# A third set of the second sequence in seven block products, with its LoRA products, sums and high and low parts moved

## What is computed

```python
# conditioning, per sequence b with its expert e = ids[b]
h = relu(x @ (wi + 2 * common_wi_b @ common_wi_a + 2 * experts_wi_b[e] @ experts_wi_a[e]).T)   # 256 -> 1024
y = h @ (wo + 2 * common_wo_b @ common_wo_a + 2 * experts_wo_b[e] @ experts_wo_a[e]).T         # 1024 -> 256
# router: the mean over the tokens decides
p = softmax(y.mean(tokens) @ gate_w); two largest, shares w = p / sum
# experts
out = x + sum over the two e of w[e] * (gelu(y @ w1[e] + b1[e]) @ w2[e] + b2[e])
```

## Time and profile before

| | us |
|---|---|
| median of 3 runs | 266.91 |
| lowest to highest | 265.99 to 267.07 |
| the profiled execution | 265.94 |
| its span, first to last instruction | 264.2 |
| PE busy | 260.0 (98%) |
| VectorE, ACT, POOL busy | 174.3, 174.8, 160.7 |
| DMA, expert weights, issue to landing (median) | 2.8 |

### The profile page before, as it was taken

One profiled execution on the slowest core, in us unless ns is written; L12 is line 12 of the kernel. 1 busy time (PEld: TensorE's weight loads), 2 busy tenths in 40 slices (PEclk: granted clock), 3 DMA queues, 4 the chain that ended last, 5 costly groups with the idle time before them and its releaser, 6 DMA issues.

```text
span 264.2 us, 3622 instructions
## 1 busy us (share of the span) xinstructions
PE 260.0 (98%) x1156; PEld 212.8 (81%) x1156; DVE 174.3 (66%) x284; ACT 174.8 (66%) x279; POOL 160.7 (61%) x192
## 2 busy tenths in 40 slices
PE   8999999999999999999999999999999999999995
PEld 4778888888878888888888888888888888888884
DVE  1882867376998636657594866658856567665665
ACT  3857365455466289888976887676777677774650
POOL 2267997933398977897549999456366366331100
PEclk9999999999999999999999999999999999999999
DMA  6987120201032102211202112203202206000004
GB/s 187 382 322 244 35 79 0 84 1 40 0 124 79 51 28 80 82 22 59 83 0 63 60 38 79 79 0 83 79 2 79 78 4 200 0 0 2 0 1 159
DMA packets 11139, 19.76 MB, mean 75 GB/s; under 512 B 2000, under 2 KB 2256, under 8 KB 10992
## 3 DMA queue, kind: packets, MB, share of 16 engines
q1 hardware_dynamic: 10544, 18.61, 21.5%
q10 hardware_dynamic: 576, 0.92, 1.0%
HBM read 17.43 MB, written 2.10 MB: 74 GB/s over the span
## 4 chain that ended last, share of the span: by engine, by line
PE 98%; DVE 0%; issue 0%
PE out_ps L762 16%; PE out_ps L759 16%; PE out_ps L758 16%; PE hid_ps L758 15%; PE hid_ps L759 14%; PE hid_ps L762 14%; PE hid_ps L959 2%; PE hid_ps L798 1%; PE out_ps L888 1%; PE hid_ps L802 1%; PE hid_ps L806 1%; PE hid_ps L910 1%; PE hid_ps L900 1%; DVE x_sb L1271 0%; DVE y_sb L1159 0%
## 5 line engine op out<-in xcount | busy, mean ns | idle before, releaser
L413 POOL TENSOR_TENSOR up_lo<-up_raw,up_hi 128x512 fp32r<-128x512 f32 x41 | 53.0, 1311 | 37.1 <-ACT up_hi L573 36.9
L758 PE MATMUL out_ps<-hid_hi,down_hi 128*128 128x512 f32 x190 | 74.0, 390 | 0.0
L762 PE MATMUL out_ps<-hid_hi,down_lo 128*128 128x512 f32 x190 | 74.0, 389 | 0.0
L759 PE MATMUL out_ps<-hid_lo,down_hi 128*128 128x512 f32 x190 | 74.0, 389 | 0.0
L758 PE MATMUL hid_ps<-act_hi,up_hi 128*128 128x512 f32 x166 | 64.9, 391 | 0.0
L759 PE MATMUL hid_ps<-act_lo,up_hi 128*128 128x512 f32 x166 | 64.7, 390 | 0.0
L762 PE MATMUL hid_ps<-act_hi,up_lo 128*128 128x512 f32 x166 | 64.6, 389 | 0.0
L605 ACT ACTIVATE hid_ps<-hid_ps,bias_sb 128x512 f32<-128x512 f32 x64 | 42.2, 659 | 29.1 <-DVE hid_ps L1080 18.0
L1054 DVE SCALAR_TENSOR_TENSOR hid_lo<-hid_ps,mix,hid_hi 128x512 fp32r<-128x512 f32 x64 | 47.9, 748 | 20.3 <-ACT hid_hi L619 19.7
L419 POOL TENSOR_TENSOR down_lo<-down_raw,down_hi 128x512 fp32r<-128x512 f32 x24 | 32.4, 1349 | 37.2 <-ACT down_hi L583 37.2
L619 ACT ACTIVATE hid_hi<-hid_ps,mix 128x512 fp32r<-128x512 f32 x64 | 44.1, 690 | 4.7
(11 more groups left out here) (98 smaller groups left out, 241.9 us busy)
## 6 DMA issues: line engine op xcount, KB each, us to landing
up_raw<-in_w SPq DMA_DIRECT2D x16, 256.0 KB, 2.8
down_raw<-in_w SPq DMA_DIRECT2D x16, 256.0 KB, 2.6
lora_raw<-in_lora SPq DMA_DIRECT2D x10, 256.0 KB, 4.8
down_raw<-in_woT SPq DMA_DIRECT2D x8, 256.0 KB, 3.8
up_raw<-in_wiT SPq DMA_DIRECT2D x7, 256.0 KB, 4.2
outT<-x_sb SPq DMA_DIRECT2D x6, 256.0 KB, 3.5
x_sb<-in_x1T SPq DMA_DIRECT2D x1, 1024.0 KB, 7.6
x_sb<-in_x0bT SPq DMA_DIRECT2D x1, 512.0 KB, 4.0
```

Of the source, the lines that this page charges most:

```text
L413: ins = eng.tensor_tensor(up_lo[:, n, cols], up_raw[:, n, cols], f32(up_hi[:, n, cols]), ALU.subtract)
L758: eng.matmul(out, w_h, a_h, start=start, stop=False, skip_group_check=onto)
L759: eng.matmul(out, w_h, a_l, start=False, stop=False, skip_group_check=onto)
L762: return eng.matmul(out, w_l, a_h, start=False, stop=stop, skip_group_check=onto)
```

## The change

Set 6 becomes a seven-product set too, so that sets 4, 5 and 6 are. What goes with it:

- The up pair of set 6 is made in set 4 (it was in set 5) and that of set 7 in set 5 (it was in set 6). VectorE's merges go with them, and the order of `PRODUCTS` with both.
- POOL makes in set 4 also the weight sums of set 6, ahead of the low part of down set 4, and the low part of up set 6, now eight blocks, directly behind it and so ahead of the router's terms and the LoRA lot of set 7. In set 5 come the first two sums of the output of sequence 0 (they waited for the router's picks and now for its maximum), the low parts of up set 7 and of down set 5. In set 6 come the other two sums, and two of the `raw_low` parts, which VectorE made.
- ACT copies in set 4 the high part of up set 6, in set 5 that of up set 7. The high parts of the output of sequence 0 (`raw_high`) and the first of its sums (`sum_high`) go from set 6 to set 5.
- VectorE makes in set 6 no `raw_low`; two stand in set 7, beside the four `sum_low`. The router's second pick and the shares stand in set 6 between the additions of the seven products.

```diff
-    PLAIN = [n for n in range(N_COND) if n not in (SETS, SETS + 1)]
+    PLAIN = [n for n in range(N_COND) if n not in (SETS, SETS + 1, SETS + 2)]
...
-    UP_FACTOR_AT = {0: [1], 1: [2], 2: [3, 4], 3: [5], 5: [6], 6: [7]}
+    UP_FACTOR_AT = {0: [1], 1: [2], 2: [3, 4], 3: [5], 4: [6], 5: [7]}
...
-    RAW_LO_AT = {2: [(0, 0), (0, 1), (0, 2), (0, 3)], 6: [(1, 0), (1, 1), (1, 2), (1, 3)],
+    RAW_LO_AT = {2: [(0, 0), (0, 1), (0, 2), (0, 3)], 7: [(1, 0), (1, 1)],
...
 # gpsimd
                 elif q == 4:
                     up_low(5)
+                    weight_sums(6)
                     down_low(4)
+                    up_low(6)
                 elif q == 5:
                     logit_terms(0)
                     term_low(0)
                     after((s_term_lo, 1))
                     lora_low(1, 4)
-                    up_low(6)
-                    down_low(5)
-                elif q == 6:
-                    eng.wait_ge(s_pick, TOP_K)
+                    eng.wait_ge(s_nmax, 1)
                     token_sum(1, 0)
                     token_sum(1, 1)
                     up_low(7)
+                    down_low(5)
+                elif q == 6:
+                    eng.wait_ge(s_pick, TOP_K)
                     token_sum(1, 2)
                     token_sum(1, 3)
+                    raw_low(eng, 1, 2)
+                    raw_low(eng, 1, 3)
                     down_low(6)
 # scalar
-                    if q - 1 in EXP_AT:
+                    if q > N_COND and q - 1 in EXP_AT:
                         up_high(q + 1)
...
                     hid_high(q, 0)
+                    if q == 5:
+                        raw_high(1, 0)
+                        raw_high(1, 1)
...
                     if seven(q):
                         hid_high(q, 1)
-                        if q > SETS:
-                            up_high(q + 1)
+                        if q + 2 < N_COND:
+                            up_high(q + 2)
+                        if q == 6:
+                            sum_high(1, 1)
                         hid_high(q, 2)
                         down_high(q)
-                    elif q == 6:
-                        raw_high(1, 0)
-                        raw_high(1, 1)
-                        up_high(7)
-                        hid_high(6, 1)
-                        down_high(6)
-                        sum_high(1, 0)
-                        hid_high(6, 2)
-                        sum_high(1, 1)
+                        if q == 5:
+                            sum_high(1, 0)
 # vector
                     second_sum(q)
                     hid_low(q - 1, 3)
+                    if q in SECOND_AT:
+                        router_second(SECOND_AT[q])
                     third_sum(q)
                     hid_low(q, 0)
+                    if q in SECOND_AT:
+                        router_shares(SECOND_AT[q])
...
-                if q in SECOND_AT:
-                    router_second(SECOND_AT[q])
...
-                if q in SECOND_AT:
-                    router_shares(SECOND_AT[q])
```

More of the change, by code:

```diff
@@ L507, in _ @@
                     lora_low(1, 4)
-                    up_low(6)
+                    eng.wait_ge(s_nmax, 1)
+                    token_sum(1, 0)
+                    token_sum(1, 1)
+                    up_low(7)
                     down_low(5)
@@ L512, in _ @@
                     eng.wait_ge(s_pick, TOP_K)
-                    token_sum(1, 0)
-                    token_sum(1, 1)
-                    up_low(7)
                     token_sum(1, 2)
                     token_sum(1, 3)
+                    raw_low(eng, 1, 2)
+                    raw_low(eng, 1, 3)
                     down_low(6)
```

## The result

| | us |
|---|---|
| kernel before, median of 22 runs | 266.90 (265.89 to 267.44) |
| changed kernel, median of 22 runs | 267.44 (266.81 to 268.31) |
| ratio, with its 95% interval | 1.0032 [1.0021, 1.0043] |
| profiled execution of the changed kernel, its span | 267.42, 265.6 |

The changed kernel is 0.3% slower, a difference that its interval sets clearly apart from none. The forecast was 267.9, or +0.37%, inside the band of 0.5%, and the range 265.9 to 269.0 holds the time.

A forecast was written before the change was run, and what follows sets the result against it. PE, busy 98% of the span, was taken as the bound. Removed work of -0.85 us and new waits of 0.9, 0.6, 0.3 and 0.1 gave +1.05, say +1.0, for a median of 267.9 us, range 265.9 to 269.0.

The forecast's parts named there:

- The work on PE: Sets 4 to 6: set 6 shorter by 1.11 us, set 4 longer by 0.26; -0.85 us with no new wait.
- The first wait: Set 5: PE's third down matmul waits for POOL's low part of down set 4, behind ACT's late copy; 0.9 us.
- the price of resuming: When PE meets a wait, it resumes 0.22 us after the end of what released it; read in set 6.
- The second wait: Set 5: PE's up pair for set 7 waits for the LoRA lot that POOL makes; 0.6 us.
- What was costed at nothing: Sets 5 and 6: ACT's y copies, POOL's down low parts, VectorE's tile sum, picks and expert loads cause no stall.
- The third wait: Set 8's start waits for VectorE's last low parts, 0.3 us; its first ACT copy adds 0.1.
- the row of 1.30: Two VectorE low parts in set 7 before took 2.61 us, 1.30 each; at that pace set 8 stalls 0.6.
- the middle between no stall and the full 0.6: Before set 8: 0.3 us taken between undisturbed low parts (0.68 each, no stall) and 1.30 each (stall 0.6).
- The sum: Whole kernel: -0.85 + 0.9 + 0.6 + 0.3 + 0.1 = +1.05 us, median 267.9.
- Rival A: The order costs nothing, POOL's sums or ACT's copy come sooner: -0.85 us, 266.1; chance 0.14.
- Rival C: Before set 8, VectorE's last three low parts each wait out a POOL operation: +3.3 us, 270.2; chance 0.25.

The follow-up runs named there:

- kernel with the lows spread: Changed kernel with ACT's up set 6 copy behind set 4's down weights and one VectorE output low part earlier in set 7; ratio 0.9959 to before.
- first experiment: Changed kernel with ACT's copy of up set 6's high part moved back behind the down weights of set 4; ratio 0.9968 to the kernel before.
- two experiments on POOL's queue: Changed kernel with router's terms and LoRA lot before up set 6's low part: ratio 1.0019; changed kernel with an extra 1.27 us operation before it: 1.0065.
- runs with three matmuls fewer: Set 6 without three low-weight matmuls, in the kernel with the lows spread (0.9969) and in the changed kernel (1.0026), ratios to the kernel before.

## Why the prediction was right

**The work on PE** (-0.85). Set 4 +0.27 for +0.26, set 6 -1.11 for -1.11. The kernel with the lows spread, in which PE meets none of the new waits, came out at -0.86.

**The first wait** (0.9). Measured 0.78. The links are where they were put: ACT's idle time ends with POOL's last sum, its down copy runs 11.20 to 11.82 after the start of set 4 (predicted 11.19 to 11.82), POOL's low part ends 13.18 after it (13.20). Half of the difference is the price of resuming: I took 0.22 us from one place of the kernel before, and here the slot comes 0.16 after the end. Most of the rest is that PE came to this matmul 12.57 after the start of the set and not 12.52. The first experiment shows the cause.

**The second wait** (0.6). Measured 0.59, and the two experiments on POOL's queue show that this queue sets its end, once ACT has delayed it. The lot ended 18.28 after the start of set 4, predicted 18.33. Together the two waits are 1.37 for 1.48: the working had held that an error in the first would be made good in the second, and it wasn't here, because PE was itself 0.07 us later at the pair than +0.24 allowed and the lot 0.05 sooner.

**What was costed at nothing** stayed at nothing in the changed kernel. The smallest cover of those (the time by which a part is ready before PE would have to wait for it) was at the low part of down set 6: it ends at 83.47, PE was due at 84.02 and would have needed it by 83.80, so 0.33 where the prediction had 0.25. The runs with three matmuls fewer show how near that was.

**The third wait** (0.3, and 0.1 in set 8). Measured 0.08 in set 7 and 0.19 in set 8, 0.27 for 0.4. By PE's slots it is 0.15 before the first matmul of set 8, 0.06 at m2, where ACT's first copy ends at 96.16 and the slot is at 96.31, and the remaining 0.06 is spread over the matmuls behind the two. Here the working was not as good as its sum. The three low parts took 3.82 us, 1.27 each, so the row of 1.30 was the right price and the middle between no stall and the full 0.6 was the wrong choice. But they began 7.15 us after the start of set 7 and not 7.6. VectorE can't begin them before it has merged down set 7, and the merge waits for PE's down pair. Before, it waited 1.11 us and the last two low parts began 7.16 after the start of the set, at 88.10; now it waits 0.51, so that the low part added ahead of it ran in idle time. The two errors offset each other. The slot of set 8's first matmul came 0.33 after the end of the last low part, more than the 0.22 of the working; why isn't shown.

**The sum.** +1.05 forecast, +0.82 measured in the stretch, and 267.9 against 267.44. The mechanism was right at both large waits; at the small third one the nearness of the sum is luck. Rival A (no cost of the order, 266.1) is the kernel with the lows spread; the change as it was made isn't that. Rival C, the port, fits the lengthened rows: one low part took 1.78 and POOL's down part beside it 1.74, where 0.68 and 1.29 are undisturbed. It came nowhere near its price of 1.29 us more for each: the three took 0.57, 1.10 and 0.27 more than 0.68, since each began with an operation of POOL already partly done. No run tried the port by itself.

## What to carry to other kernels

Where an engine's queue is strictly in order, the place of a step can matter more than its length: a copy of 1.05 us, wanted by PE 13 us later, cost 1.4 us because it stood two places too early and waited for another engine, with nearer work behind it. Put a step behind the work that is due sooner, and ahead of a wait ask what stands in the queue after it. And when an edit saves less than the run-to-run spread, compare the same stretch of two traces, from one matmul to another; here it repeated to 0.01 us in the one kernel that was profiled twice.

## What the runs showed of the hardware

I had not expected how much the start differs from one execution to the next. The twelve warm-up matmuls, ahead of anything that the change touches, first in the kernel before, then in the changed one:

```profile
1.20 4.10 PE L959 MATMUL hid_ps<-y_sb 128*128 128x512 bf16 x12 [1.20 <-DVE y_sb L1159]
```

```profile
1.20 4.83 PE L962 MATMUL hid_ps<-y_sb 128*128 128x512 bf16 x12 [1.20 <-DVE y_sb L1162]
```

They begin at the same time and take 0.73 us longer, and all that follows up to set 4 is later by that much. Over the ten profiles set 4 starts between 47.91 and 49.30. This spread is larger than the effect under study. Two parts of it can be seen. The weight loads of the warm-up stand 0.43 us apart until 3.73 in both kernels; before, the last four then follow within 0.75 us from 4.06 on, and in the changed kernel they stay 0.42 to 0.43 apart until 5.43. The profile's clock column shows 1.00 in both. And in the kernel with the copy moved back, where the warm-up took 4.05 us, PE then waited 0.76 us for the load of `lora_first`. What decides when the pace changes wasn't tried.
